# Projecting queries, keys and the feed-forward layer of two sequences at once, in three f32r products of 256 columns

## The reference

```
L0: q = x Wq + bq;  k, v = ctx Wk + bk, ctx Wv + bv      # 16 heads of 8, ctx has 77 rows
    x = LayerNorm(x + softmax(clip(q k^T / sqrt(8) * (0.5 mask + 0.5))) v Wo + bo)
L1: xn = rms_norm(x);  q, k, v = split(xn @ to_qkv_w)    # 128 x 3072, 16 heads of 64
    q, k = rope(q), rope(k)
    keys = memory token, 16 persistent, 64 of the own segment, causal
    x = x + softmax(q keys^T / 8) values @ to_out_w
    h = rms_norm(x) @ ff_w1 + b1;  a, g = split(h)       # 128 x 682
    x = x + (silu(g) * a) @ ff_w2 + b2                   # 341 x 128
```

## Time and profile before

| | |
|---|---|
| median of 3 runs | 1434.27 us (1434.16 to 1435.74) |
| the profiled execution, its time | 1432.96 us |
| its span, from the first to the last instruction | 1431.2 us |
| TensorE busy | 1381.2 us |
| VectorE busy | 1043.6 us |
| GpSimd busy | 817.5 us |
| ScalarE busy | 790.7 us |
| mean granted clock of TensorE | 0.993 |

### The profile page before, as it was taken

How to read it: one execution, slowest core, us unless ns; L and a number is a source line. 1 busy time by engine, 2 the same in 40 slices (tenths; PEclk the granted TensorE clock), 3 DMA queues, 4 the chain that set the end, 5 groups by cost and what they waited for, 6 DMA issues and landing times.

```text
span 1431.2 us, 54338 instructions
## 1 busy us (share of the span) xinstructions
PE 1381.2 (97%) x20771; PEld 1220.9 (85%) x20771; DVE 1043.6 (73%) x3025; ACT 790.7 (55%) x1933; POOL 817.5 (57%) x1169
## 2 busy tenths in 40 slices
PE   2699999999999999999999999999999999999996
PEld 1588898898898888888889889889888888888986
DVE  4567777777777777777777777777777777777763
ACT  1346556556556555655655655655655565565553
POOL 1445655655655665665565565565566566556553
PEclk9889999999999999999999999999999999999999
DMA  6432322222232232222232222223223222223210
GB/s 186 122 102 73 101 102 76 97 102 80 92 104 86 89 101 91 86 101 102 72 101 102 72 100 102 78 95 103 87 87 103 92 86 101 99 75 101 102 42 30
DMA packets 106145, 133.13 MB, mean 93 GB/s; under 512 B 16309, under 2 KB 88522, under 8 KB 105994
## 3 DMA queue, kind: packets, MB, share of 16 engines
q1 hardware_dynamic: 106122, 132.81, 28.1%
HBM read 41.04 MB, written 24.61 MB: 46 GB/s over the span
## 4 chain that ended last, share of the span: by engine, by line
PE 95%; DMA 2%; DVE 1%; ACT 1%; SPq 0%; issue 0%; POOL 0%; POOLq 0%; ACTq 0%; DVEq 0%
PE psum L927 17%; PE psum L963 12%; PE psum L976 10%; PE psum L1006 9%; PE psum L990 6%; PE psum L969 5%; PE psum L983 5%; PE psum L940 5%; PE psum L1121 4%; PE psum L934 4%; PE psum L954 2%; PE psum L920 2%; PE psum L921 2%; PE psum L922 2%; PE psum L1042 2%; PE psum L1019 2%
## 5 line engine op out<-in xcount | busy, mean ns | idle before, releaser
L620 ACT ACTIVATE probs<-psum 81x512 f32<-81x512 f32 x256 | 151.0, 591 | 283.8 <-PE psum L969 283.8
L927 PE MATMUL psum<-xnT,wqkv 128*128 128x128 f32 x2048 | 267.3, 279 | 0.0
L737 DVE TENSOR_TENSOR ra<-psum,rope 128x512 f32<-128x512 f32 x256 | 174.7, 683 | 100.7 <-PE psum L927 100.7
L927 PEld LDWEIGHTS psum<-xnT,wqkv 128*128 128x128 f32 x2048 | 246.9, 194 | 0.2 <-ACT xnT L568 0.2
L537 POOL TENSOR_TENSOR ug<-tanh_gate,half_gate 128x384 f32<-128x384 f32 x64 | 64.2, 1003 | 281.3 <-ACT half_gate L611 281.3
L500 POOL TENSOR_SCALAR z<-z 77x512 f32<-77x512 f32 x256 | 156.7, 621 | 99.6 <-DVE z L742 99.6
L742 DVE TENSOR_TENSOR z<-psum,wT 77x512 f32<-77x512 f32 x256 | 163.6, 680 | 42.8 <-PE psum L934 42.8
L963 PE MATMUL psum<-qT,kall 64*81 64x64 f32 x4096 | 177.2, 237 | 0.0
L746 DVE TENSOR_REDUCE mx<-psum 128x4 f32<-128x324 f32 x256 | 119.5, 488 | 78.0 <-PE psum L954 78.0
L963 PEld LDWEIGHTS psum<-qT,kall 64*81 64x81 f32 x4096 | 159.5, 149 | 18.0 <-issue 12.5
L737 DVE TENSOR_TENSOR rb<-psum,rope 128x512 f32<-128x512 f32 x256 | 174.0, 680 | 0.0
(11 more groups left out here) (137 smaller groups left out, 2577.9 us busy)
## 6 DMA issues: line engine op xcount, KB each, us to landing
rs<-rb SPq DMA_DIRECT2D x256, 256.0 KB, 2.4
qk_dram<-qk_parts SPq DMA_DIRECT2D x64, 307.5 KB, 4.1
qk_stack<-qk_dram SPq DMA_DIRECT2D x256, 76.9 KB
seq_in<-in SPq DMA_DIRECT2D x64, 166.5 KB
out<-out_sb SPq DMA_DIRECT2D x64, 64.0 KB, 1.6
maskT<-in SPq DMA_DIRECT2D x64, 38.5 KB
vall<-memv_dram SPq DMA_DIRECT2D x128, 4.0 KB, 1.9
ctx_all<-in SPq DMA_DIRECT2D x5, 320.0 KB, 6.1
```

Of the source, the lines that this page charges most:

```text
L620: return nc.scalar.activation(probs[:, 4 * t:4 * t + 4, :].rearrange("k n i -> k (n i)"), at(f"score{t}")[0:KEYS, :], ACT.Exp, scale=float ...
L737: last = V.tensor_tensor(dst[:, place(name)].rearrange("p (c i) -> p c i", c=4), p, rope[:, n, :].unsqueeze(1).broadcast_to([128, 4, S]), ...
L927: last = mm(at(name)[:, S * n:S * (n + 1)], wqkv[:, lo + 128 * n:lo + 128 * (n + 1)], xnT[:])
```

## The change

A body now handles two sequences in each stage, and `LEAD = 8`: 36 bodies run, n = -8, -6, ..., 62. In body n the sequences n + 8 and n + 7 get their cross projections, the pair n + 5 and n + 4 the query and key projections in one go, n + 3 and n + 2 the self attention, n + 1 and n the feed-forward layer. Four bodies (-8 to -2) are partly filled, 28 (0 to 54) are full, and four (56 to 62) are emptying.

Weights and activations of the query, key and feed-forward projections are split into a float32r `hi` and `lo`, like the values' before. A product for two sequences at once is three passes of 256 columns: hi by hi, hi by lo, lo by hi. Query and key projections have eight banks a pair instead of four a sequence. The splitting of the weights (now 3072 + 682 columns instead of 1024) is done once, at the start, ScalarE the `hi`, GpSimd the `lo`. The feed-forward layer has three bank fills a pair: `both` (the 85 last features of gate and lin), `gate` and `lin`. `hnT` gets `hi` and `lo` tensors, made by ScalarE and GpSimd. The temporary tensors of the start (contexts, `wqkv`, tables) now lie inside `rot` and `rs`. The order of the work in a body and the banks are new on every engine.

```diff
-LEAD = 4
-QK = ("q0", "k0", "q1", "k1")
+LEAD = 8
+QK = ("q0", "k0", "q1", "k1", "q2", "k2", "q3", "k3")
...
-            ("q1", 4, 2, (q1_rotated,)),
+            ("k0", 5, 5, (k0_rotated,)),
...
+            ("v0.0", 5, 4, (v0_kept,)),
...
-            for n in range(-LEAD, 1):
+            for n in range(-LEAD, 1, 2):
                 turn(n)
-            with eng.Fori(1, B - LEAD) as n:
+            with eng.Fori(2, B - LEAD - 1, 2) as n:
                 turn(n)
-            for n in range(B - LEAD, B + 0):
+            for n in range(B - LEAD, B, 2):
                 turn(n)
...
+            def product(dst, columns, w_hi, w_lo, hi, lo, start=True):
+                mm(dst, w_hi[:, columns], hi, start=start, stop=False)
+                mm(dst, w_hi[:, columns], lo, start=False, stop=False)
+                return mm(dst, w_lo[:, columns], hi, start=False)
...
             def project_turned(name):
-                lo = INNER * "qk".index(name[0]) + BANK * int(name[1])
-                for n in range(4):
-                    last = mm(at(name)[:, S * n:S * (n + 1)], wqkv[:, lo + 128 * n:lo + 128 * (n + 1)], xnT[:])
+                for n in range(2):
+                    lo = INNER * "qk".index(name[0]) + 128 * (2 * int(name[1]) + n)
+                    last = product(at(name)[:, 2 * S * n:2 * S * (n + 1)], slice(lo, lo + 128), wqkv_hi, wqkv_lo, xT_hi, xT_lo, start=n == 0)
                 return last
...
-            def into_ff(name, part):
-                for n in range(FCH):
-                    lo = DFF * part + 128 * n
-                    last = mm(at(name)[0:FROWS[n], S * n:S * (n + 1)], w1[:, lo:lo + FROWS[n]], hnT[:])
-                return last
+            def into_ff(dst, part, n):
+                lo = DFF * part + 128 * n
+                return product(dst, slice(lo, lo + FROWS[n]), w1_hi, w1_lo, hT_hi, hT_lo)
...
+                    if first(seq[4]):
+                        pe.wait_ge(w_in, WEIGHTS_IN)
+                        pe.wait_ge(w_lo_ready, 2)
+                    free(pe, "k0", n, 5)
+                    pe.wait_ge(xnT_lo_ready, done[6])
+                    project_turned("k0").then_inc(k0_filled, 2)
```

More of the change, by code:

```diff
@@ L352, in free @@
                 _, _, ahead, read = users[(place - back) % len(users)]
[L353 removed]
+                turn = ahead + 2 * ((place - back) // len(users))
                 if live(n, turn) is not None:
@@ L993, in body @@
             def body(n, seq, done):
                 if seq[1] is not None:
-                    if first(seq[1]):
+                    free(pe, "oT0.1", n, 1)
+                    pe.wait_ge(o0_ready, done[2])
+                    turn_heads(1, 0).then_inc(oT0_filled, 1)
+                if seq[5] is not None:
+                    free(pe, "pv.1", n, 5)
+                    pe.wait_ge(u_kept, done[6])
+                    for g in range(GROUP):
+                        last = nc.tensor.transpose(at("pv.1")[:, S * g:S * (g + 1)], u[:, S * g:S * (g + 1)], ident[:])
+                    last.then_inc(pv_filled, 1)
@@ L996, in body @@
+                if seq[1] is not None:
+                    free(pe, "out.1", n, 1)
+                    pe.wait_ge(oT1_ready, done[2])
+                    for i in range(PAIRS):
+                        last = mm(at("out.1")[:, 0:D], oT[:, i, :], wout[:, i, :], start=i == 0, stop=i == PAIRS - 1)
+                    last.then_inc(out_filled, 1)
+                if seq[2] is not None:
+                    if first(seq[2]):
                         pe.wait_ge(setup_act, 4)
                         pe.wait_ge(consts_cast, 1)
-                    free(pe, "max2", n, 1)
@@ new lines, in body @@
+                if seq[0] is not None:
+                    free(pe, "down.0", n, 0)
+                    pe.wait_ge(sT_ready, done[2])
+                    for i in range(FCH):
+                        last = mm(at("down.0")[:, 0:D], sT[0:FROWS[i], i, 0, :], w2[0:FROWS[i], i, :], start=i == 0, stop=i == FCH - 1)
+                    last.then_inc(down_filled, 1)
+                if seq[7] is not None:
+                    free(pe, "qkv.1", n, 7)
+                    pe.wait_ge(inputs_in, done[8] * 32)
+                    p = at("qkv.1")
@@ new lines, in body @@
+                if seq[3] is not None:
+                    free(pe, "v1.1", n, 3)
+                    project("v1.1").then_inc(v1_filled, 1)
+                if seq[5] is not None:
+                    free(pe, "xnT", n, 5)
+                    pe.wait_ge(xn_ready, done[6])
+                    for c in range(2):
+                        last = nc.tensor.transpose(at("xnT")[:, S * c:S * (c + 1)], xn[:, c, :], ident[:])
+                    last.then_inc(xnT_filled, 2)
+                    if first(seq[4]):
+                        pooled_tokens()
```

1339 lines of the change are left out of this document (850 added, 489 removed).

## The result

The changed kernel takes 1440.09 us (median of 6 runs, 1438.45 to 1443.79), the kernel before beside it 1433.63 us (median of 6). The ratio is 1.0046, with a 95% interval of 1.0032 to 1.0061. The forecast was 1375 us. The profiled execution has a span of 1437.0 us.

What follows compares the result with a forecast made beforehand. TensorE's own work was taken to bound the full bodies. Start 124 + 28 x 40.3 + end 120 gave a 1372 us span, 1374 for an execution, 1375 with the median's 1.3 above the profiled run; range 1346 to 1408.

Steps and rivals of the forecast that it cites:

- The passes: TensorE's 256-column float32r passes: 0.118 us each, bounds 0.112 and 0.129; 66 a pair take 7.79 us, saving 2.3.
- cheap: Rival: passes at 0.112 us and a first full body near 110 us, giving 1348 us; chance 0.14.
- dear rival: Rival: a 256-column pass costs much more than half a 512-column one, gain gone from 0.149 us; chance 0.05.
- TensorE's work in a body: TensorE's own work in a full body of two sequences: 40.2 us.
- The body: Length of a full two-sequence body: 40.3 us, 39.9 to 40.9, including VectorE late by 0 to 0.5 us.
- one stretch of VectorE, from `k0` to `o0_ready`: VectorE's rotations, masked products and normalisations: 13.3 us, 13.8 with overheads, against 13.4 of TensorE's own way.
- covered: Rest of the body: `hn` chain has over 4 us of other TensorE work; GpSimd's eight sums run beside TensorE's work.
- The rival with VectorE or GpSimd as the bound: Late hand-over to VectorE's stretch makes TensorE wait 1 to 2 us in 28 bodies: 1403 to 1431 us; chance 0.18.
- the prediction's own signs of being wrong: Body 0 starting after 140 us, a body over 41 us with TensorE idle in it, or passes dearer than 0.13.
- The start: Time before the first full body: near 124 us, 31 later than before, bounds 105 and 135.
- The end: Bodies 56 to 62, emptying: together 120 us, against 65.0 before.
- cost next to nothing: Start's 31 us and end's 55 are about the 85 us of four sequences leaving the middle; the gain is the bodies'.

Runs made afterwards that it cites:

- accum_max: Changed kernel with `hn` in accumulator form, the weights' lower parts made one body earlier, and heads 3's maxima ahead of `x1`'s mean square: 1399.9 us, ratio 0.9768.
- gpsimd_waits: Changed kernel with one more wait on GpSimd, ahead of q2's rotary sum, until `hn` of the pair's first sequence is written: 1430.4 us, ratio 0.9986.
- hn_product: Changed kernel with the first sequence's `hn` in its place but computed by `tensor_tensor` with the factor broadcast, instead of `tensor_scalar`: 1455.4 us, ratio 1.0139.
- max_first: Changed kernel with `hn` moved behind q2's rotary products, the weights' lower parts one body earlier, heads 3's maxima ahead of `x1`'s mean square: 1405.0 us, ratio 0.9806.
- input_first: max_first with SyncE's loads of the third sequence's input and mask put ahead of the other weights' six loads: 1404.3 us, ratio 0.9790.

## Why the prediction was wrong

**The passes: right.** Starts of the 256-column passes lie 0.117 to 0.120 us apart at full clock (0.118 forecast), so neither the cheap nor the dear rival came true.

**TensorE's work in a body: right.** 40.04 us against 40.2.

**The body: this step failed.** The prediction checked one stretch of VectorE, from `k0` to `o0_ready`, and that one was right (VectorE's timeline of the changed kernel, its first and last row):

```profile
712.34 3.68 DVE L920 TENSOR_TENSOR rot<-psum,rope 128x512 f32<-128x512 f32 x6 [1.43 <-PE psum L1206]
...
725.24 0.42 DVE L940 TENSOR_TENSOR o<-psum,rden 128x256 f32<-128x256 f32 x1
```

It lasts 13.3 us, as forecast, and no product of TensorE waits for `o` in a body, only a weight load by 0.17 us. All else was "covered", with `hn` "over 4 us of other TensorE work" away from its use and "GpSimd's eight sums" running "beside the next body's first transposes". It took VectorE's durations from a kernel in which none of the 64 `hn` was held out (279 to 285 ns), and placed one of each pair beside three of those sums. The rival with VectorE or GpSimd as the bound (0.18) had the size, 1 to 2 us a body, but other places and reasons, and its 1403 to 1431 us leave out the longer ends. Measured: 1.12 us at the bank and 0.26 for the first heads' weights. Three experiments on `hn` (place, form, a gap in the sums) each took its 3.9 us down to 0.27 to 0.33, and the accumulator form and the maxima first together brought the body to 40.23, near the forecast's 40.3. Two of the prediction's own signs of being wrong came true, body 0 after 140 us and a body over 41 us with TensorE idle in it.

**The start: mis-sized by 23 us, in all its terms.** Forecast: transposes at 63, tokens to 70, first projection 79, q2 summed 93, body 0 at 124 (its terms add up to 125). Measured: 68.1, 80.7, 91.5, 110.3 (109.05 + 1.26) and 147. The steps are 5, 6, 2, 5 and 6 us too short. In two of them the rows show something that was left out, which is a part of the 23 us and not all of it. The first projections come after 9.69 us without work and run at half speed, 0.21 us apart (91.85 to 92.06) instead of 0.118. And the centring beside the sums is held out there too, 2.12 us instead of 0.35 (up to 4.6 us in other kernels of this study). The lower parts' 8.3 us were forecast rightly and could be moved off the path; that experiment gave 7.7 us.

**The end: mis-sized by 11 us.** Forecast 39.5, 35, 28 and 18; measured 41.3, 38.8, 28.2 and 22.7, by the output product's starts at 1307.9, 1349.2, 1388.0 and 1416.2, the last up to the span's end and with the 1.9 us that a body has ahead of this product (1306.0 to 1307.9). The first two carry the held-out `hn` (40.1 and 37.7 in accum_max). The last is a chain with nothing beside it: two gating products of 1.26 us each on GpSimd, passes at half clock, and the second output waiting 1.72 us for the first one's store. This part was read from the trace and not tested.

**The sum.** 147 + 28 x 41.39 + 131 = 1437. The prediction said that the ends "cost next to nothing" beyond the 85 us of the four sequences that leave the middle. They grew by 278 - 158.4 = 120 us, so they cost 35 us, while the bodies gained 28 x (42.43 - 41.39) = 29. That is the 6 us by which the kernel became slower. With accum_max's repairs the bodies gain 28 x 2.2 = 62 and the ends cost 269.2 - 158.4 - 85 = 26, 36 us together, as its span shows (1431.2 to 1395.7). What is still missing to the forecast's 1372 is the start's 15.5 and the end's 9.7 us.

## What to carry to other kernels

When a change reorders two engines, list for each stretch in which GpSimd works back to back what VectorE does on SBUF alone beside it: a duration taken from the old neighbourhood does not hold in the new one, and a busy engine may be one that stands still. Repair by place, by form (an accumulator output; `x1`, with one operand in PSUM, was not held out either) or by a gap on GpSimd, and put what frees a bank ahead of what may be held out; one repair alone gave 0.2 to 0.6 of the 1.2 us a body, since the next instruction was held out in its turn, or TensorE met its next wait. A body for two sequences pays in the middle and costs at both ends, so the ends need terms of their own, with TensorE at half clock for part of them.

## What the runs showed of the hardware that was not expected

- A held-out instruction of VectorE is not served between two sums that follow each other: `hn` was issued at 727.83 during k2's sum and finished after q1's, three sums later (3.94 us). With a gap of 0.26 us behind k2's sum it took 0.27 us.
- The mean square in gpsimd_waits was issued 0.05 us before the end of one sum (727.34 against 727.39) and stood through the whole next one: 1.42 us.
- Of the same 128x128 product beside the sums, `tensor_scalar` and `tensor_tensor` took 3.5 us in the mean, `tensor_scalar` with an accumulator output 0.33 us.
- 1.2 us without work on TensorE was followed by a stretch at a granted clock of 0.50 in 9 of 28 bodies of hn_product, which made six of them 1.1 to 1.2 and three 2.6 to 4.1 us longer than its others.
- In the start, from 100 to 120 us, the granted clock was 0.80 in max_first's execution and 0.53 in input_first's, and 2.3 us gained ahead of that stretch were gone behind it.
